# The down product of a mixture-of-experts layer in three fp32r products, with its weights split anew for each tile

## The chip, the cores and the metric

One Trainium2 chip (trn2), one of its cores, one launch. The metric is the device time of that core in microseconds (us), measured over the whole program. All times here are such device times, or spans of one profiled execution of the program.

## The reference

A block of cross-attention followed by a mixture of experts, all in fp32, over 32 sequences of 112 tokens (3584 tokens) of width 256:

```
x = x + attention(layernorm(x), ctx)          # 16 heads of 64, 375 context rows of 192
h = layernorm(x)
p = softmax(h @ gate_w)                       # 8 experts; the best two per token
for each expert e:
    gate, up = split(h @ gate_up_w[e])        # 256 -> 2 x 512
    out_e = (silu(gate) * up) @ down_w[e]     # 512 -> 256
x = x + sum over the two chosen experts of share * out_e
```

The change touches the last product, `@ down_w[e]`, alone.

## The kernel before

The program has two stages. The first walks over the sequences in pairs (`pair`), with attention, the second layernorm, the router, and a scatter of each token's row, twice, into the `bins` of its two experts in memory. The second (`four_tiles`, from about 1158 us on) walks over 63 tiles of 128 rows; all rows of a tile belong to one expert, whose number is read into registers from the table `tile_expert`. `over_tiles` (L187) writes the first twelve tiles out, then loops four tiles at a time, then writes out the last; each engine runs its own copy of `four_tiles`, and semaphores alone order the engines among each other. On each engine the instructions run in the order in which they are written.

The weights of all experts lie in SBUF. Those of gate and up (`Wgu`) are held in two fp32r parts: a high part (the value rounded to fp32r) and a low part (the remainder). A product of two operands so split is made as three matmuls, high by high, high by low and low by high, all into one accumulator (`split_product`, L1314). `Wd`, the down weights, is held whole, in fp32.

For a tile t the engines do this:

- SyncE (SP) reads the tile's first row from the table and loads its 128 rows (`load_rows`, L567), three tiles ahead.
- TensorE (PE) turns the rows into columns (`turn_rows`, L1573, 2 transposes), ScalarE (ACT) rounds them into `hT_h` (`hi_of_rows`, L905), VectorE (DVE) writes the remainder into `hT_l` (`lo_of_rows`, L1245) and keeps the tile's destinations and shares (`keep_dest`, L1251).
- PE makes gate and up (`gate`, L1593, and `hidden`, L1587), 6 matmuls of 512 columns each, with moving operands addressed by the expert's register.
- ACT takes silu of gate out of PSUM (L923); DVE multiplies it with up into `hid` (L1282).
- PE transposes `hid` (L1622, 4 transposes), DVE copies it out of PSUM as `hidT` (L1274), and PE makes the down product in fp32: four matmul instructions, which the profile shows as eight (L1638).
- ACT scales the result by the token's share into `y_out` (L931), and GpSimd (POOL) adds the rows to the output in memory by an indirect DMA (L779). Each of these waits until the one before has landed, since two tiles can hold the same token.

On PE one pass of the loop, for tile t, has this order: transposes of `hid` of t-1; rows of t+1; up of t; down of t-1; gate of t+1. On ACT: silu of t, rounding of the rows of t+1, `y_out` of t-1. On DVE: copy of `hidT` of t-1, remainder of the rows of t+1, `keep_dest`, `hid` of t. `down_ps`, the accumulator of the down product, is one bank; `gate_ps` and `up_ps` are two banks each, `hidT_ps` and the bank of the turned rows are one each.

The first tiles begin before the router is through with the last two sequences. What is left of them, and the rest of the table of tiles (`tiles_left`, `experts_left`, `rows_left`, L1146 to L1176), is written between the tiles, one piece per tile, at given tile numbers.

Of the kernel before, what the change touches and what calls it, by code (L numbers as in the profile page):

```python
# [201 lines left out]
def attention_and_experts(nc, x, ctx_in, Wq, Wkv, Wproj, bproj, gate_w, gate_up_w, down_w, out):  # L202
# [4 lines left out]
    with ExitStack() as stack:  # L207
# [126 lines left out]
        hid = sb("hid", [P, FF], F32)  # L334
        hidT = sb("hidT", [P, FJ, P], F32)
        y_out = sb("y_out", [P, 2, C], F32)
        plan2_at = place["at"]
# [14 lines left out]
        assert place["at"] <= scratch_at + 2 * NJ * C * 4  # L352
# [55 lines left out]
        gate_made, up_made, silu_done, hid_done = sem("gate_made"), sem("up_made"), sem("silu_done"), sem("hid_done")  # L408
        hidT_made, hidT_done, down_made, y_done = sem("hidT_made"), sem("hidT_done"), sem("down_made"), sem("y_done")
# [35 lines left out]
        def _(sp):  # L445
# [153 lines left out]
        def _(pool):  # L599
# [170 lines left out]
            def four_tiles(i):  # L770
                for k in range(4):
# [10 lines left out]
                    if known(t) and t == 3:  # L782
                        scatter(B - 2, 0, None)
                    if known(t) and t == 7:
# [6 lines left out]
        def _(act):  # L791
# [123 lines left out]

            def four_tiles(i):
                for k in range(4):
                    t = 4 * i + k
                    if there(t, NT):
                        act.wait_ge(gate_made, t + 1)  # L920
                        if not known(t) or t >= 1:
                            act.wait_ge(hid_done, t)
                        nc.scalar.activation(silu[:], gate_ps[k % 2][:], ACT.Silu).then_inc(silu_done, 1)  # L923
                    if there(t + 1, NT) and not (known(t) and t == 0):
                        hi_of_rows(t + 1, (k + 1) % 2)
# [7 lines left out]
                    if known(t) and t == 4:  # L933
                        open_gates(B - 1, C_ps)

# [3 lines left out]
        def _(dve):  # L939
# [328 lines left out]

            def four_tiles(i):
                for k in range(4):  # L1270
                    t = 4 * i + k
                    if there(t - 1, NT):
                        dve.wait_ge(hidT_made, t)
                        nc.vector.tensor_copy(hidT[:].rearrange("p j n -> p (j n)"), hidT_ps[:]).then_inc(hidT_done, 1)  # L1274
                    if there(t + 1, NT) and not (known(t) and t == 0):
                        lo_of_rows(t + 1, (k + 1) % 2)

                        keep_dest(t + 1, 2 * i + (k - 3) // 2 + 1, (k + 1) % 4)
                    if there(t, NT):
                        dve.wait_ge(silu_done, t + 1)  # L1280
                        dve.wait_ge(up_made, t + 1)
# [3 lines left out]
                    if known(t) and t == 1:  # L1285
# [4 lines left out]
                    if known(t) and t == 3:  # L1290
                        keep_hnT(B - 1, C_ps)
                    if known(t) and t == 4:
                        least(B - 1, C_ps)
                    if known(t) and t == 5:
# [382 lines left out]
```

## Time and profile before

| | us |
|---|---|
| median of three runs | 1499.28 (1498.85 to 1500.79) |
| the profiled execution | 1500.38 |
| its span | 1498.6 |
| PE busy in the span | 1461.8 (98%) |
| DVE, ACT, POOL busy | 950.6, 732.1, 550.7 |
| granted clock of PE, mean | 0.994 of full speed |

"Busy" of PE is modelled from pipelined matmuls whose times overlap, so what a group of matmuls costs is better read from the distance between starts, or from its piece in the chain of waits. "PEld" is PE's loading of weights, which overlaps its matmuls. A name with a q behind the engine (PEldq, SPq) is the engine's own queue: register, branch and semaphore instructions and DMA issues, which are not counted as busy. "L931" is line 931 of the kernel.

### The profile page before, as it was taken

How to read it: one execution, taken by the hardware profiler on the slowest of the kernel's cores; microseconds unless marked ns; L12 is line 12 of the kernel's file. 1: busy time of each engine (PE TensorE's matmuls, PEld its weight loads, DVE VectorE, ACT ScalarE, POOL GpSimd, SP SyncE). 2: the span in 40 equal slices, each digit the busy share in tenths (PEclk: the TensorE clock that was granted, in tenths of full speed). 3: DMA queues.
4: the chain of work that ended last, by engine and by line, in shares of the span. 5: the costliest groups of instructions: out<-in, count | busy, mean ns of one | idle time of the engine just before them, and what ended most of it. 6: DMA issues, size and time to landing. Idle time of an engine off the chain costs nothing.

```text
span 1498.6 us, 37285 instructions
## 1 busy us (share of the span) xinstructions
PE 1461.8 (98%) x11882; PEld 1289.0 (86%) x11883; DVE 950.6 (63%) x2600; ACT 732.1 (49%) x2032; POOL 550.7 (37%) x641
## 2 busy tenths in 40 slices
PE   6999999999999999999999999999997999999997
PEld 5888889888888988898889888888886888888886
DVE  5667777677767776767777777767668543333332
ACT  4555555555555555555555555555556322222221
POOL 3424334343434343433334343434354332233222
PEclk9999999999999999999999999999998999999999
DMA  9222222222222222222222222213027233333332
GB/s 253 86 66 68 74 73 72 68 73 66 72 72 72 75 92 80 76 72 66 72 73 72 69 72 66 76 40 108 29 80 260 56 59 54 51 49 50 52 53 25
DMA packets 101105, 113.80 MB, mean 76 GB/s; under 512 B 17244, under 2 KB 88140, under 8 KB 101068
## 3 DMA queue, kind: packets, MB, share of 16 engines
q1 hardware_dynamic: 87900, 94.33, 20.6%
q0 software_dynamic: 12144, 15.66, 6.4%
q10 hardware_dynamic: 1024, 3.34, 0.7%
q8 instruction: 21, 0.34, 0.1%
q14 instruction: 16, 0.13, 0.0%
HBM read 61.37 MB, written 51.93 MB: 76 GB/s over the span
## 4 chain that ended last, share of the span: by engine, by line
PE 94%; DVE 3%; DMA 1%; issue 1%; ACT 0%; POOLq 0%; DVEq 0%; SPq 0%
PE bank L1375 25%; PE bank L1318 17%; PE bank L1444 11%; PE bank L1420 10%; PE bank L1410 9%; PE bank L1638 7%; PE bank L1465 6%; PE bank L1382 4%; PE bank L1622 2%; PE bank L1577 1%; DVE probT L1187 1%; DVE Wgu L1056 1%; PE bank L1492 1%; DMA WqL_whole<-in_L_xattn_Wq 1%; PE bank L1482 0%
## 5 line engine op out<-in xcount | busy, mean ns | idle before, releaser
L844 ACT ACTIVATE prob<-bank,neg_max 112x375 f32<-112x375 f32 x512 | 298.7, 588 | 135.7 <-DVE neg_max L1181 135.7
L1181 DVE TENSOR_REDUCE neg_max<-bank 112x1 f32<-112x375 f32 x512 | 243.7, 538 | 16.0 <-PE bank L1410 15.9
L1420 PE MATMUL bank<-ident,prob 112*125 112x112 f32 x1536 | 214.5, 273 | 2.7 <-ACT prob L844 2.4
L1420 PEld LDWEIGHTS bank<-ident,prob 112*125 112x125 f32 x1536 | 195.9, 188 | 13.8 <-ACT prob L844 4.8
L779 POOL DMA_INDIRECT out<-y_out,dest_now x63 | 98.1, 1557 | 221.6 <-ACT y_out L931 196.5
L1444 PE MATMUL bank<-probT,V 125*64 125x112 f32 x3072 | 176.5, 264 | 1.9 <-DVE probT L1187 1.1
L1318 PE MATMUL bank<-Wgu,hT_h 128*128 x504 | 177.1, 433 | 1.0 <-DVE hT_l L1247 1.0
L1444 PEld LDWEIGHTS bank<-probT,V 125*64 125x64 f32 x3072 | 149.0, 137 | 28.4 <-issue 25.1
L969 DVE TENSOR_TENSOR K_l<-bank,K_h 128x376 fp32r<-128x376 f32 x256 | 140.2, 549 | 51.6 <-ACT K_h L804 45.3
L959 DVE COPY V<-bank 125x512 f32<-125x512 f32 x96 | 66.4, 692 | 137.7 <-PE bank L1382 134.7
L802 ACT COPY V<-bank 125x512 f32<-125x512 f32 x96 | 56.3, 587 | 181.3 <-PE bank L1382 178.7
L682 POOL CAST OT_h<-O_now 128x448 fp32r<-128x448 f32 x64 | 37.3, 583 | 287.9 <-DVE O_now L1033 282.0
L1274 DVE COPY hidT<-bank 128x512 f32<-128x512 f32 x63 | 43.5, 691 | 154.4 <-PE bank L1622 154.4
L804 ACT CAST K_h<-bank 128x376 fp32r<-128x376 f32 x256 | 120.9, 473 | 30.6 <-PE bank L1375 29.0
L1187 DVE COPY probT<-bank 125x336 f32<-125x336 f32 x256 | 121.2, 494 | 0.1
L1638 PE MATMUL bank<-Wd,hidT 128*128 x504 | 119.2, 379 | 1.5 <-DVE hidT L1274 1.5
L850 ACT COPY probT<-bank 125x336 f32<-125x336 f32 x256 | 100.3, 443 | 33.5 <-PE bank L1420 33.0
L931 ACT ACTIVATE y_out<-bank,share_now 128x256 f32<-128x256 f32 x63 | 29.8, 473 | 176.9 <-PE bank L1638 176.9
L1375 PE MATMUL bank<-yA_h,WkH 128*128 128x376 f32 x256 | 99.4, 388 | 13.0 <-DVE WkU L987 13.0
L1638 PEld LDWEIGHTS bank<-Wd,hidT 128*128 128x128 f32 x504 | 95.3, 189 | 17.0 <-issue 2.0
L844 ACT ACTIVATION_READ_ACCUMULATOR prob<-bank,neg_max 112x1 f32 x512 | 108.2, 211 | 0.0
L717 POOL TENSOR_SCALAR std<-mv 112x1 f32<-112x1 f32 x32 | 7.7, 240 | 271.8 <-DVE mv L1050 271.8
(196 smaller groups left out, 3587.8 us busy)
## 6 DMA issues: line engine op xcount, KB each, us to landing
bins<-pad_rows SPq DMA_DIRECT2D x29, 1032.0 KB, 5.8
inv_rows<-sums SPq DMA_DIRECT2D x126, 128.0 KB, 2.8
h_in<-bins SPq DMA_DIRECT2D x63, 129.0 KB, 2.1
Wgu<-in_L_ffn_gate_up_w SPq DMA_DIRECT2D x6, 1024.0 KB, 7.8
y_sb<-in_ctx SPq DMA_DIRECT2D x32, 187.5 KB, 2.6
y_sb<-in_ctx SPq DMA_DIRECT2D x62, 93.8 KB, 2.6
x_sb<-in_x SPq DMA_DIRECT2D x16, 224.0 KB, 2.9
x_res<-in_x SPq DMA_DIRECT2D x32, 112.0 KB, 2.4
```

The costliest lines, as they stand in the source:

```text
L804: nc.scalar.copy(K_h[:, arg, :], src[:, 0:LKE]).then_inc(hi_done, 1)
L844: nc.scalar.activation(prob[:, j, :], S_ps[j][0:LQ, 0:LKV], ACT.Exp, bias=neg_max[:, j:j + 1], accum_out=row_sum[:, head // HB, head % HB: ...
L850: nc.scalar.copy(probT[:, j, :], S_ps[j][0:KR, 0:KT * LQ]).then_inc(probT_second, 1)
L969: nc.vector.tensor_tensor(lo, ps, hi.bitcast(F32), ALU.subtract).then_inc(lo_done, 1)
L1181: nc.vector.tensor_reduce(neg_max[:, j:j + 1], S_ps[j][0:LQ, 0:LKV], AX.X, ALU.max, negate=True).then_inc(max_done, 1)
L1187: nc.vector.tensor_copy(probT[:, j, :], S_ps[j][0:KR, 0:KT * LQ]).then_inc(probT_first, 1)
L1318: last = mm(dst, w, m, start=n == 0, stop=n == len(todo) - 1)
L1375: last = mm(out, w, y, start=begins and n == 0, stop=ends and n == "both")
L1410: last = mm(S_ps[2 * k + r][0:LQ, 0:LKE], w[rows, p, q], m[rows, p, :], start=n == 0, stop=n == len(todo) - 1)
L1420: last = nc.tensor.transpose(S_ps[j][0:KR, t * LQ:t * LQ + LQ], prob[:, j, t * KR:t * KR + KR], ident[0:LQ, 0:LQ])
L1444: last = mm(O_ps[r * DK:r * DK + DK, c:c + LQ], V[:, t, (2 * p + r) * DK:(2 * p + r) * DK + DK], probT[:, 2 * k + r, t * LQ:t * LQ + LQ], ...
L1638: last = mm(down_ps[:, 0:C], hidT[:, j, :], Wd[:, experts[k], j, :], start=j == 0, stop=j == FJ - 1)
```

## The change

`hidT` and the down weights are split into fp32r parts, and the down product is made by `split_product` (12 matmuls). ACT writes the high part of `hidT` out of PSUM, DVE the low part. Since there is no room for a second copy of all of `Wd`, the tile's expert is split anew for each tile, high part by ACT, low part by DVE, into one of two buffers, `down_even` and `down_odd`, which lie over memory that attention no longer needs. For this both engines read the experts' numbers into registers, four at a time. `hid` is written in place of silu, so silu of a tile waits for the transposes of the tile before.

The order within a pass changes too. PE: rows of t+1; transposes of `hid` of t-1; up of t; gate of t+1; down of t-1. ACT: rounding of the rows of t+1; high part of `hidT` of t-1; silu of t; high part of the weights of t; `y_out` of t-1. DVE: low part of the rows of t+1; low part of `hidT` of t-1; `keep_dest`; `hid` of t; low part of the weights of t. The pieces of the router and of the plan move one tile later. The plan's temporaries (`plan2_at`) move behind `down_even`.

```diff
@@ -331,10 +331,16 @@
         Wgu = sb("Wgu", [P, E, 2, 2, 2 * FF], F32R)
         scratch_at = place["at"]
         silu = sb("silu", [P, FF], F32)
-        hid = sb("hid", [P, FF], F32)
-        hidT = sb("hidT", [P, FJ, P], F32)
+        hidT_h = sb("hidT_h", [P, FJ, P], F32R)
+        hidT_l = sb("hidT_l", [P, FJ, P], F32R)
         y_out = sb("y_out", [P, 2, C], F32)
-        plan2_at = place["at"]
+        down_parts = [None, nc.alloc_sbuf_tensor_at("down_odd", [P, 2, FJ, C], F32R, offset=place["at"])]
+        assert place["at"] + 2 * FJ * C * 4 <= scratch_at + 2 * NJ * C * 4
+        even_at = plan_at + HALF * P * 4
+        down_parts[0] = nc.alloc_sbuf_tensor_at("down_even", [P, 2, FJ, C], F32R, offset=even_at)
+        plan2_at = even_at + 2 * FJ * C * 4
         h_in = nc.alloc_sbuf_tensor_at("h_in", [P, 4, W], F32, offset=h_in_at)
         place["at"] = wd_at
...
@@ -913,16 +920,38 @@
             hi_of_experts(7, E)
             nc.scalar.activation(table[:], ident[:, 0:1], ACT.Silu)
 
+            def experts_from(i):
+
+                c = 4 * i + 1
+                return nc.values_load_multi_w_load_instructions(
+                    tile_expert[0:1, c:c + 4] if known(i) else tile_expert[0:1, bass.ds(c, 4)],
+                    engines=(mybir.EngineType.Activation,), min_val=0, max_val=E - 1)[1]
+
             def four_tiles(i):
+                if known(i) and i == 0:
+                    act.wait_ge(plan, N_PLAN1)
+                experts = experts_from(i)
                 for k in range(4):
                     t = 4 * i + k
+                    if there(t + 1, NT) and not (known(t) and t == 0):
+                        hi_of_rows(t + 1, (k + 1) % 2)
+                    if there(t - 1, NT):
+                        act.wait_ge(hidT_made, t)
+                        if not known(t) or t >= 2:
+                            act.wait_ge(down_made, t - 1)
+                        nc.scalar.copy(hidT_h[:].rearrange("p j n -> p (j n)"), hidT_ps[:]).then_inc(hidT_hi, 1)
                     if there(t, NT):
                         act.wait_ge(gate_made, t + 1)
                         if not known(t) or t >= 1:
-                            act.wait_ge(hid_done, t)
+                            act.wait_ge(hidT_made, t)
                         nc.scalar.activation(silu[:], gate_ps[k % 2][:], ACT.Silu).then_inc(silu_done, 1)
-                    if there(t + 1, NT) and not (known(t) and t == 0):
-                        hi_of_rows(t + 1, (k + 1) % 2)
+                        if known(t) and t == 0:
+                            act.wait_ge(proj_made, B)
+                            act.wait_ge(wd_early, 16)
+                            act.wait_ge(wd_in, 16)
+                        if not known(t) or t >= 2:
+                            act.wait_ge(down_made, t - 1)
+                        nc.scalar.copy(down_parts[k % 2][:, 0], Wd[:, experts[k]]).then_inc(wd_hi, 1)
                     if there(t - 1, NT):
                         act.wait_ge(down_made, t)
                         if not known(t) or t >= 3:
...
-                    if known(t) and t == 4:
+                    if known(t) and t == 5:
                         open_gates(B - 1, C_ps)
+                    if known(t) and t == 11:
+                        act.wait_ge(plan, N_PLAN)
...
             def four_tiles(i):
+                experts = experts_from(i)
                 for k in range(4):
                     t = 4 * i + k
-                    if there(t - 1, NT):
-                        dve.wait_ge(hidT_made, t)
-                        nc.vector.tensor_copy(hidT[:].rearrange("p j n -> p (j n)"), hidT_ps[:]).then_inc(hidT_done, 1)
                     if there(t + 1, NT) and not (known(t) and t == 0):
                         lo_of_rows(t + 1, (k + 1) % 2)
-
+                    if there(t - 1, NT):
+                        dve.wait_ge(hidT_hi, t)
+                        nc.vector.tensor_tensor(hidT_l[:].rearrange("p j n -> p (j n)"), hidT_ps[:],
+                                                hidT_h[:].rearrange("p j n -> p (j n)").bitcast(F32),
+                                                ALU.subtract).then_inc(hidT_done, 1)
+                    if there(t + 1, NT) and not (known(t) and t == 0):
                         keep_dest(t + 1, 2 * i + (k - 3) // 2 + 1, (k + 1) % 4)
                     if there(t, NT):
                         dve.wait_ge(silu_done, t + 1)
                         dve.wait_ge(up_made, t + 1)
-                        nc.vector.tensor_tensor(hid[:], up_ps[k % 2][:], silu[:], ALU.mult).then_inc(hid_done, 1)
-                    if known(t) and t == 0:
+                        nc.vector.tensor_tensor(silu[:], up_ps[k % 2][:], silu[:], ALU.mult).then_inc(hid_done, 1)
+                        dve.wait_ge(wd_hi, t + 1)
+                        nc.vector.tensor_tensor(down_parts[k % 2][:, 1], Wd[:, experts[k]],
+                                                down_parts[k % 2][:, 0].bitcast(F32), ALU.subtract).then_inc(wd_lo, 1)
+                    if known(t) and t == 1:
                         residual(NP, B - 1, 1, C_ps)
...
+                    if known(t) and t == 8:
                         tiles_left()
-                    if known(t) and t == 8:
+                    if known(t) and t == 9:
                         experts_left()
-                    if known(t) and t == 9:
+                    if known(t) and t == 10:
                         rows_left()
...
                     if known(t) and t == 1:
                         pe.wait_ge(gates_done, B - 1)
                         hidden(up_ps[k % 2][:], experts[k + 1], k % 2, 1).then_inc(up_made, 1)
+                    if there(t + 1, NT) and not (known(t) and t == 0):
+                        turn_rows(i if k < 3 else i + 1, t + 1, (k + 1) % 4)
                     if there(t - 1, NT):
                         pe.wait_ge(hid_done, t)
                         if not known(t) or t >= 2:
                             pe.wait_ge(hidT_done, t - 1)
                         for j in range(FJ):
-                            last = nc.tensor.transpose(hidT_ps[:, j * P:j * P + P], hid[:, j * P:j * P + P], ident[:])
+                            last = nc.tensor.transpose(hidT_ps[:, j * P:j * P + P], silu[:, j * P:j * P + P], ident[:])
                         last.then_inc(hidT_made, 1)
-                    if there(t + 1, NT) and not (known(t) and t == 0):
-                        turn_rows(i if k < 3 else i + 1, t + 1, (k + 1) % 4)
                     if there(t, NT) and not (known(t) and t == 1):
                         if not known(t) or t >= 2:
                             pe.wait_ge(hid_done, t - 1)
                         hidden(up_ps[k % 2][:], experts[k + 1], k % 2, 1).then_inc(up_made, 1)
+                    if there(t + 1, NT):
+                        gate(t + 1, experts[k + 2], (k + 1) % 2)
                     if there(t - 1, NT):
                         pe.wait_ge(hidT_done, t)
-                        if known(t) and t == 1:
-                            pe.wait_ge(wd_early, 16)
-                            pe.wait_ge(wd_in, 16)
+                        pe.wait_ge(wd_lo, t)
                         if not known(t) or t >= 2:
                             pe.wait_ge(y_done, t - 1)
-                        for j in range(FJ):
-                            last = mm(down_ps[:, 0:C], hidT[:, j, :], Wd[:, experts[k], j, :],
-                                      start=j == 0, stop=j == FJ - 1)
-                        last.then_inc(down_made, 1)
-                    if there(t + 1, NT):
-                        gate(t + 1, experts[k + 2], (k + 1) % 2)
-                    if known(t) and t == 2:
+                        parts = down_parts[(k + 1) % 2]
+                        split_product(down_ps[:, 0:C], [(hidT_h[:, j, :], hidT_l[:, j, :], parts[:, 0, j, :], parts[:, 1, j, :])
+                                                        for j in range(FJ)]).then_inc(down_made, 1)
+                    if known(t) and t == 3:
                         count(B - 2)
```

## Rows read from the trace of the kernel before

**Rows 1.** Page of the kernel before: busy time by engine, and the chain's shares.
```profile
PE 1461.8 (98%) x11882; PEld 1289.0 (86%) x11883; DVE 950.6 (63%) x2600; ACT 732.1 (49%) x2032; POOL 550.7 (37%) x641
...
PE 94%; DVE 3%; DMA 1%; issue 1%; ACT 0%; POOLq 0%; DVEq 0%; SPq 0%
```

**Rows 2.** Chain of waits, 1463 to 1499 us: start, duration (us), what.
```profile
1470.54 1.41 PE bank L1318 x6
1471.94 0.44 PE bank L1622 x4
1472.38 0.22 PE bank L1577 x2
1472.60 1.40 PE bank L1318 x6
1474.00 1.73 PE bank L1638 x8
```

**Rows 3.** Page: costliest groups: times | busy us, mean ns | idle before.
```profile
L1638 PE MATMUL bank<-Wd,hidT 128*128 x504 | 119.2, 379 | 1.5 <-DVE hidT L1274 1.5
```

**Rows 4.** Timeline of all engines, 1440 to 1447 us: start, us, engine, line, [idle before].
```profile
1439.61 0.47 ACT L931 ACTIVATE y_out<-bank,share_now 128x256 f32<-128x256 f32 x1 [2.89 <-PE bank L1638]
...
1440.88 0.60 ACT L923 ACTIVATE silu<-bank 128x512 f32<-128x512 f32 x1 [0.79 <-PE bank L1318]
...
1441.32 0.69 DVE L1274 COPY hidT<-bank 128x512 f32<-128x512 f32 x1 [2.81 <-PE bank L1622]
1441.54 0.37 ACT L907 CAST hT_h<-bank 128x256 fp32r<-128x256 f32 x1
...
1441.94 0.42 DVE L1247 TENSOR_TENSOR hT_l<-bank,hT_h 128x256 fp32r<-128x256 f32 x1
```

**Rows 5.** Chain of waits, 608 to 616 us: the output projection.
```profile
611.00 2.85 PE bank L1465 x24
```

**Rows 6.** Instructions of lines 814, 1056 and 684: ns min/median/max, first and last start.
```profile
L814 ACT CAST Wgu<-Wgu x6: 1894/1900/1912, 1128.5 to 1157.2; 128x2048 fp32r<-128x2048 f32 x6
...
L1056 DVE TENSOR_TENSOR Wgu<-Wgu x6: 2281/2292/3037, 1147.0 to 1160.6; 128x2048 fp32r<-128x2048 f32 x6
...
L684 POOL TENSOR_TENSOR OT_l<-O_now,OT_h x64: 1127/1139/3052, 55.5 to 1149.8; 128x448 fp32r<-128x448 f32 x64
```

**Rows 7.** Register loads: PE's queue at line 1583 (1220 to 1222.5 us), SP's at 568.
```profile
L1583 PEldq SEQ_ASSERT  x4: 18/18/18, 1221.2 to 1222.0; - x4
L1583 PEldq TENSOR_LOAD <-tile_expert x1: 338/338/338, 1220.6 to 1220.6; - x1
...
L568 SPq TENSOR_LOAD <-tile_row x2: 265/265/265, 1230.1 to 1235.3; - x2
```

**Rows 8.** Timeline of ACT and DVE, side work in the first tiles.
```profile
1185.47 1.28 ACT L855 ACT_TABLE_LOAD   x1
...
1186.88 0.27 ACT L855 ACTIVATE gates<-bank,neg_top 112x8 f32<-112x8 f32 x1
...
1190.41 0.16 DVE L1073 MAX8 top<-gates 112x8 f32<-112x8 f32 x1
...
1191.69 0.16 DVE L1096 TENSOR_SCALAR dest<-dest 112x2 f32<-112x2 f32 x1
...
1210.33 0.29 DVE L1166 TENSOR_REDUCE prev<-t_tc 128x18 f32<-128x144 f32 x1
...
1212.32 0.18 DVE L1175 SCALAR_TENSOR_TENSOR tile_row<-e_of,within 128x18 int32<-128x18 f32 x1
```

**Rows 9.** Line 779: time from issue to landing; timeline of the last tiles.
```profile
DMA to landing us min/median/max: 3.5/3.8/3.9
...
1487.20 1.56 POOL L779 DMA_INDIRECT out<-y_out,dest_now  x1 [3.42 <-ACT y_out L931]
1489.21 0.47 ACT L931 ACTIVATE y_out<-bank,share_now 128x256 f32<-128x256 f32 x1 [2.82 <-PE bank L1638]
1491.94 1.55 POOL L779 DMA_INDIRECT out<-y_out,dest_now  x1 [3.18 <-issue]
```

More of the change, by code:

```diff
@@ L577, in four_tiles @@
                     t = 4 * i + k
-                    if known(t) and t == 1:
+                    if known(t) and t == 2:
                         sp.wait_ge(x2_done, B)
@@ L781, in four_tiles @@
                             y_out[:, (k + 1) % 2, :], None, compute_op=ALU.add).then_inc(y_store[(k + 1) % 2], 16)
-                    if known(t) and t == 3:
+                    if known(t) and t == 4:
                         scatter(B - 2, 0, None)
-                    if known(t) and t == 7:
+                    if known(t) and t == 8:
                         scatter(B - 1, 1, None)
@@ L1267, in _, with experts_from @@
                 lo_of_expert(e)
+            def experts_from(i):
+                c = 4 * i + 1
+                return nc.values_load_multi_w_load_instructions(
+                    tile_expert[0:1, c:c + 4] if known(i) else tile_expert[0:1, bass.ds(c, 4)],
+                    engines=(mybir.EngineType.DVE,), min_val=0, max_val=E - 1)[1]
             def four_tiles(i):
+                experts = experts_from(i)
                 for k in range(4):
                     t = 4 * i + k
-                    if there(t - 1, NT):
-                        dve.wait_ge(hidT_made, t)
-                        nc.vector.tensor_copy(hidT[:].rearrange("p j n -> p (j n)"), hidT_ps[:]).then_inc(hidT_done, 1)
                     if there(t + 1, NT) and not (known(t) and t == 0):
                         lo_of_rows(t + 1, (k + 1) % 2)
+                    if there(t - 1, NT):
[4 more added lines that the diff above has]
+                    if there(t + 1, NT) and not (known(t) and t == 0):
                         keep_dest(t + 1, 2 * i + (k - 3) // 2 + 1, (k + 1) % 4)
@@ L1281, in four_tiles @@
                         dve.wait_ge(up_made, t + 1)
[L1282 to L1283 removed]
+                        nc.vector.tensor_tensor(silu[:], up_ps[k % 2][:], silu[:], ALU.mult).then_inc(hid_done, 1)
[3 more added lines that the diff above has]
+                    if known(t) and t == 1:
                         residual(NP, B - 1, 1, C_ps)
[L1285 removed]
+                    if known(t) and t == 2:
                         choose(B - 2)
                         mark(B - 2, 0)
[L1288 removed]
+                    if known(t) and t == 3:
                         assign(B - 2, 0)
[L1290 removed]
+                    if known(t) and t == 4:
                         keep_hnT(B - 1, C_ps)
[L1292 removed]
+                    if known(t) and t == 5:
                         least(B - 1, C_ps)
[L1294 removed]
+                    if known(t) and t == 6:
                         choose(B - 1)
                         mark(B - 1, 1)
[L1297 removed]
+                    if known(t) and t == 7:
                         assign(B - 1, 1)
[L1299 removed]
+                    if known(t) and t == 8:
                         tiles_left()
[L1301 removed]
+                    if known(t) and t == 9:
                         experts_left()
[L1303 removed]
+                    if known(t) and t == 10:
                         rows_left()
```

14 lines of the change are left out of this document (6 added, 8 removed).

## The prediction

> **What bounds the kernel now.** I read the page first: TensorE (PE) carries 98% of the span and 94% of the chain [rows 1]. So the question is what PE does per expert tile, and whether anything else ever makes it wait. The chain of waits over the expert stage answers the first half: it never leaves PE, and repeats the five pieces of [rows 2] at each tile. Gate 1.41, transposes of hid 0.44, transposes of the next rows 0.22, up 1.40, down 1.73: 5.20 us (5.18 to 5.19 from start to start). The down product has eight matmuls per tile, 504 in 63 tiles [rows 3]. The timeline of the other engines shows how far they are from PE: VectorE (DVE) idles 2.8 us before it copies hidT, ScalarE (ACT) 2.9 us before y_out [rows 4]. PE is the bound; a cheaper down product comes through in full, as long as the new order leaves PE fed.
>
> **The down product.** Removed: eight fp32 passes, 1.73 us [rows 2]. Added: twelve matmuls of 256 columns on fp32r parts. The output projection is the same form: 24 in 2.85 us, 0.119 each [rows 5], so 1.42 for twelve. Its weights have 112 columns, those here 128; the transposes of hid load 128 columns for each matmul and keep a pace of 0.11 [rows 2], so weight loading does not set the pace. Bounds: 0.11 each (1.32) and 0.216 as now (2.59, if fp32r brought nothing). I take 1.42: 0.31 less per tile. It holds for tiles 0 to 60 (61 times): **-18.9 us**. The new tile is 4.88 us.
>
> **New work on ACT and DVE.** hidT is now rounded by ACT (512 columns, as silu: 0.60) and the remainder taken by DVE (0.69, as the copy it replaces) [rows 4, 6]. The down weights: 1024 columns. Between silu's 0.597 for 512 and the 1.900 for 2048 on ACT a straight line gives 1.03; between DVE's 0.691 and 2.281 it gives 1.22 [rows 4, 6]. ACT then works 0.37+0.60+0.60+1.03+0.47 = 3.07 us of 4.88, DVE 0.42+0.69+0.69+1.22 = 3.02 and two copies of one column. Enough room by sum; what counts is the order.
>
> **One tile, from the end of the down product (time 0).** y_out takes ACT to 0.49. The rows' transposes are out at 0.22, so ACT rounds the rows 0.53 to 0.90, DVE subtracts 0.94 to 1.36 (0.47, 0.37 and 0.42 from [rows 4]). The gate product waits for this. PE arrives there after 0.22+0.44+1.40 = 2.06, its first matmul some 0.15 earlier because matmuls overlap: **0.5 us of slack**. Before, gate stood behind down and had 1.73 more. Then hidT: ACT 0.93 to 1.53, DVE 1.57 to 2.26, needed by down at 3.4; silu to 2.15, rounded weights to 3.2, hid 2.5 to 3.2, weight remainder 3.25 to 4.5, needed in the next tile at 3.4. Slack above 1 us everywhere else. The up product wants hid of the tile before last, long done. PE's new wait for the weight remainder has the whole next tile queued behind it, but the remainder is three us early; ACT's new waits for the down product of the tile before last are met before it comes to them. silu now waits for the transposes of hid (one buffer): out at 0.66, costs nothing.
>
> **Register loads.** Every four tiles ACT and DVE must fetch four expert numbers. PE's own group runs from 1220.6 to 1222.0, 1.4 us; SP's loads have 0.265 instead of 0.338 us for the fetch itself [rows 7]. On DVE it hides behind the weight remainder. On ACT it stands ahead of the rounding of rows, the one chain with little slack. If ACT's queue runs on while y_out computes, rounding starts at some 1.3 to 1.6 instead of 0.53, and PE waits 0.3 to 0.6; if it only starts after y_out, 1.1; if ACT does it for free, 0. I take 0.45, since each of these loads is a queue instruction and y_out's wait is behind the queue by then. There are 15 such starts (t = 4 to 60): **+6.7 us**, bounds 0 and +16.5. The Trainium skill, "DMA: Bandwidth & Descriptors", Latency and other measured facts, gives such a fetch a floor of about 600 ns; by it the wait would be about 0.7, an estimate, and the sum 4 us more. The trace has fetches of 0.265 and 0.338, below that floor, and they decide.
>
> **Side work in the first tiles.** The changes of tile number keep each piece where its input is made. DVE has 1.3 us before the next rows plus the 0.5 of slack, so pieces up to 1.8 us fit. The eight steps for rows_left, 2.17 us [rows 8], do not: 0.3 late. The exponential for the last sequence needs another table: load 1.28 and 0.27 of work between y_out and the rounding of rows [rows 8]: gate waits 1.0. Silu's own load follows, the weight remainder ends 2.5 us later than usual, and choose with mark (1.44 from first to last [rows 8]) stands behind it and ahead of the next rows: 1.3 more. DVE's register loads behind assign, twice: 0.9 together. Sum **+3.5 us**, bounds +1 and +6. Start: gate of tile 2 now covers the splitting of hidT of tile 0, so that the first down loses a wait: -0.3. The wait for Wd moves from PE to ACT, 6 us earlier, its transfer was issued ahead of those of the last experts that ACT had already split; no cost.
>
> **End.** Tile 61's down must wait for the two steps of hidT with only up (1.40) before it: +0.1. The last tile's chain is longer by ACT's 0.6 and shorter by down's 0.3, but the last scatter starts 4.74 us after the one before (1487.20 to 1491.94), while y_out was out at 1489.68 [rows 9]. With POOL's usual 0.8 us after y_out, 1.4 us of cover remain, no cost.
>
> **Sum.** -18.9 + 6.7 + 3.5 - 0.3 + 0.1 = -8.9 us. The profiled execution took 1500.4 (span 1498.6), so it would take 1491.5; the median of the runs is 1499.3, 1.1 lower, hence **1490.4**.
>
> **Rivals.**
> Full gain (25%): ACT's queue loads cost nothing, or slack is larger. For it: queues run ahead on PE without a gap in the chain. Against: ACT's wait for the down product blocks its queue first. -18.9+3.5-0.2 = -15.6: 1483.7; with cheap side work 1481.
> Loads in full (12%): each four-tile start costs 1.1 us: -18.9+16.5+3.5-0.2 = +0.9: 1500.2, no change.
> Scatter as the bound (6%): a scatter cycle (3.5 to 3.9 to landing, then about 0.9 to the next start [rows 9]) is 4.74, against 4.88. It caps any further gain at 0.45 per tile; if it took 4.95, -0.24 x 61 = -14.6 before the other terms: 1494.7.
> Slower, by the weight remainder on DVE (10%): its two SBUF inputs hold up POOL, as the 2048-column subtraction of the expert weights may have done to POOL's OT_l (1.14 usually, 3.05 at most, the last one, which ran beside it) [rows 6]. If 1.22 us of it fell on each scatter's descriptors, the cycle would be 5.96 us, 0.77 over today's tile: +47, 1546. It decides from 0.45 us of overlap on. POOL runs from 1.35 to 2.9 of the tile, the remainder from 3.25 to 4.5: 0.35 us apart, so it needs POOL to slip first. The Trainium skill, "SBUF — State Buffer", Who interferes with whom, has a vector instruction with two SBUF inputs contend only with a GpSimd instruction that reads SBUF, and infers that descriptor writing is spared. By that rule this rival costs nothing; no row of before shows such an instruction beside the scatter.
> A milder slower case (5%): another 0.8 us or more in ACT's chain in every tile (waits, addresses from registers) would eat the slack and the 0.31: 1500 to 1515.
> The change not doing what it says (weights loaded no faster than 0.19 each, twelve of them, 2.27 us) is spoken against by [rows 2, 5]; 1%.
>
> **Numbers.** Forecast's own case 41%: 1486 to 1496. Range 1481 to 1501 leaves out the slower rivals and the far edge of the full gain. Measurement of this kernel can tell 0.2%, 3 us. Faster: own case, full gain, scatter and a part of the loads in full, 0.75; within 3 us 0.10, most of the rest of that case; slower 0.15, from the slower rivals.
>
> **What would show it.** The chain: the down product as x12 at 1.42; tiles of 4.88 with one of about 5.3 in four, its wait on gate behind DVE hT_l behind ACT hT_h, behind register loads on ACT's queue. One wait of 1 us after the second table load. ACT copies of Wd near 1.03, DVE near 1.22. Wrong if all tiles are alike; if down's pace is not 0.119; if the scatter's idle time is released by its own landing in most tiles; if scatter instructions grow beyond 1.55.

## The result and the profile after

The changed kernel takes **1513.36 us** (median; 1512.75 to 1513.77) against 1500.03 for the kernel before on the same chip: a ratio of 1.0084, 95% interval 1.0071 to 1.0097. Forecast was 1490.4, range 1481 to 1501. The change makes the kernel slower by 13 us, and the forecast had the wrong sign.

The page of the changed kernel: PE is busy 13 us less than in [rows 1], in a span that is 13 us longer. The gate's matmuls, which waited 1.0 us in all before (its line stands first below, and is L1318 there), now idle 25.2 us for the low part of the rows.

```profile
L1318 PE MATMUL bank<-Wgu,hT_h 128*128 x504 | 177.1, 433 | 1.0 <-DVE hT_l L1247 1.0
```

After:

```profile
PE 1448.6 (96%) x12134; PEld 1285.2 (85%) x12135; DVE 1027.1 (68%) x2664; ACT 813.4 (54%) x2159; POOL 555.9 (37%) x641
...
L1362 PE MATMUL bank<-Wgu,hT_h 128*128 x504 | 167.9, 415 | 25.2 <-DVE hT_l L1278 25.2
...
L1278 DVE TENSOR_TENSOR hT_l<-bank,hT_h 128x256 fp32r<-128x256 f32 x63 | 26.7, 424 | 111.6 <-ACT hT_h L914 109.4
```

The chain of waits shows both halves of the story. `split_product` makes gate, up and down alike (L1362), so one piece now holds twenty-four matmuls: up 1.40, gate 1.40 and down 1.42, together 4.23 us (in run 3 below up and gate alone take 2.81, which leaves 1.42).

```profile
1259.47 0.22 PE bank L1621 x2
1259.68 0.44 PE bank L1668 x4
1260.12 4.23 PE bank L1362 x24
...
1269.42 0.05 ACT y_out L960
...
1269.84 0.91 ACTq L926
...
1271.85 0.38 ACT hT_h L914
1272.26 0.44 DVE hT_l L1278
...
1272.82 3.08 PE bank L1362 x18
```

A tile is 0.22+0.44+4.23 = 4.89 us, against 5.19 in [rows 2]; forecast was 4.88. The down product does what it should. But once in four tiles the chain leaves PE: y_out, then ScalarE's queue (ACTq) at L926, the register loads, then the rounding and the remainder of the rows, and only then gate. From 1251.48, where one such gate starts, to 1272.82 for the next, four tiles take 21.34 us; at 4.88 they would take 19.52. So each passage through the head of the loop costs 1.8 us. Before, four tiles took 20.74.

Most of it is idle time of TensorE, here in the timeline of the passage at 1312 us:

```profile
1315.49 0.73 PE L1362 MATMUL bank<-Wgu,hT_h 128*128 x2 [1.49 <-DVE hT_l L1278]
```

The other 0.3 us stands at no instruction of its own. Gate and down take 3.08 us in the chain behind this wait and 2.82 otherwise, so I read it as the overlap between matmuls that a wait breaks.

What the loads take is in the view of each line, the number of instructions and their minimum/median/maximum ns. ScalarE's line:

```profile
L926 ACTq FUSED_REGOPS  x64: 147/150/170, 1158.5 to 1484.4; - x64
...
L926 ACTq TENSOR_LOAD <-tile_expert x16: 900/912/1117, 1157.4 to 1482.8; - x16
```

and VectorE's:

```profile
L1303 DVEq TENSOR_LOAD <-tile_expert x16: 967/1268/1377, 1160.7 to 1480.6; - x16
```

A fetch is 0.912 us on ScalarE and 1.268 on VectorE. On SP it is 0.265 [rows 7]. The 0.338 of [rows 7] for PE is only one of its two kinds: in the kernel before, its fetches of four numbers take 0.329 to 0.345 us and most of those of two numbers about 0.54; all together give

```profile
L1583 PEldq TENSOR_LOAD <-tile_expert x33: 329/487/615, 1156.2 to 1474.3; - x33
```

The fetch and the register instructions for its four numbers make a group that ends 1.93 us after it begins. It stands wholly behind the start of y_out, and behind the loop's own register work (L192). In the chain of one pass of the loop:

```profile
1312.19 0.04 ACTq L192
...
1312.41 0.07 ACTq L192
...
1312.51 0.91 ACTq L926
...
1314.44 0.04 ACTq L913
```

The down product ends at 1311.94 there, so the fetch begins 0.57 us behind it, and the rounding of the rows 2.58 us behind it. The last pass is written out, and all but one of the loop's instructions are gone from it. Its down product ends at 1482.46, and the fetch begins 0.32 us behind it:

```profile
1482.71 0.04 ACTq L192
...
1482.78 0.91 ACTq L926
```

That long tile is 1.4 us too long and not 1.8: y_out of tiles 58 and 59 come 6.11 us apart, and 4.74 where run 4 below has no loads.

The first tiles are slow too. Reading y_out in the timeline of each kernel: it comes for tile 0 at 1170.78 (before: 1169.11), for tile 10 at 1226.69 (before: 1221.78). Ten tiles at the new pace should have taken 49 us and took 56.

```profile
1170.43 0.42 DVE L1074 TENSOR_TENSOR x<-bank,x_bias 112x256 f32<-112x256 f32 x1
...
1171.87 0.25 POOL L724 TENSOR_SCALAR std<-mv 112x1 f32<-112x1 f32 x1 [20.28 <-DVE mv L1081]
...
1176.09 1.69 POOL L786 DMA_INDIRECT out<-y_out,dest_now  x1 [0.17 <-issue]
```
```profile
1180.69 1.22 DVE L1325 TENSOR_TENSOR down_odd<-Wd,down_odd 128x1024 fp32r<-128x1024 f32 x1
...
1180.83 2.53 POOL L786 DMA_INDIRECT out<-y_out,dest_now  x1 [3.05 <-DVE share_now L1287]
```

The residual of the last sequence, one tile later than before, holds up GpSimd's (POOL's) normalisation by 6.7 us (std at 1171.87; before 1165.13), and the first scatter with it: 1176.09 against 1170.52. The second scatter begins just behind the weight remainder on VectorE (L1325) and takes 2.53 us instead of 1.55. So do the two after it (2.57 and 2.52).

VectorE's own register loads stand in the chain as well, ahead of the remainder of the rows. They take 1.95 us here (1182.66 to 1184.61), and 1.93 once more from 1206.29 on:

```profile
1182.66 0.84 DVEq L1303
...
1184.66 0.42 DVE hT_l L1278
```

The end gains nothing. Behind tile 60 the last two y_out come 1.2 us sooner than before, but the scatters are behind: the last one starts 4.0 us after the last y_out instead of 2.7, and the chain closes over two landings in a row. From y_out of tile 60 to the end it is 17.9 us, before 17.7.

```profile
1494.92 4.25 DMA out<-y_out,dest_now
...
1500.05 3.77 DMA out<-y_out,dest_now
```

### The profile page after: what moved, and what is told of

Same layout as the page of the kernel before. It is cut to its first block and busy times, and to the rows that moved or that the text cites. A ratio compares the mean times of both kernels' runs of the same rounds, so it can differ in the third digit from the quotient of the medians.

```text
span 1511.5 us, 38193 instructions
## 1 busy us (share of the span) xinstructions
PE 1448.6 (96%) x12134; PEld 1285.2 (85%) x12135; DVE 1027.1 (68%) x2664; ACT 813.4 (54%) x2159; POOL 555.9 (37%) x641
## 5 line engine op out<-in xcount | busy, mean ns | idle before, releaser
L1362 PE MATMUL bank<-Wgu,hT_h 128*128 x504 | 167.9, 415 | 25.2 <-DVE hT_l L1278 25.2
L1362 PEld LDWEIGHTS bank<-Wgu,hT_h 128*128 128x128 f32 x504 | 90.3, 191 | 49.6 <-issue 33.4
L1278 DVE TENSOR_TENSOR hT_l<-bank,hT_h 128x256 fp32r<-128x256 f32 x63 | 26.7, 424 | 111.6 <-ACT hT_h L914 109.4
L1362 PE MATMUL bank<-Wgu,hT_l 128*128 x252 | 100.2, 398 | 0.0
```

Of the source, the lines that this page charges most:

```text
L1362: last = mm(dst, w, m, start=n == 0, stop=n == len(todo) - 1)
```

## The experiments

Each run is compared with the kernel before on the same chip (medians of 1499.0 to 1500.5 in all batches).

**1. ScalarE's loads moved.** Behind the first silu of a pass, ahead of the first weight copy:

```diff
-                experts = experts_from(i)
                 for k in range(4):
...
                         nc.scalar.activation(silu[:], gate_ps[k % 2][:], ACT.Silu).then_inc(silu_done, 1)
+                        if k == 0:
+                            experts = experts_from(i)
```

> The changed kernel with one thing moved: ScalarE reads its four expert numbers after the first silu of a pass of four tiles, in front of the first weight copy, instead of ahead of the rounding of rows. Theory A (the register loads at the head of the pass hold up rows, and so gate): the long tile of each four shrinks from 6.66 to about 4.9 us, four tiles take 19.6 instead of 21.32, the sum of 15 passes gives back 24 to 27 us, 1487 to 1490. Rival B (the branch of the loop and what it costs on each engine, or the scatter, makes the long tile): four tiles stay at 21.3, 1513. Rival C (with the loads out of the way the scatter chain or the weight remainder binds): four tiles stop at 20 to 20.7, 1495 to 1505.

Six executions fell in two groups: 1490.38, 1491.01 and 1491.78, and 1525.56, 1526.67 and 1527.64. The lower ones against before: 0.9939 (0.9920 to 0.9959). They are theory A: 22 us come back from moving one read, a little under the 24 to 27 expected. The upper group is a thing of its own, and the profile fell on it. Waits, then the timeline around one scatter:

```profile
DVE dest_now L1287 <- DMA out<-y_out,dest_now: 116.9, 49, 2.8
```
```profile
1301.27 0.15 DVE L1287 CAST dest_now<-h_in 128x1 int32<-128x1 f32 x1 [2.52 <-DMA out<-y_out,dest_now]
...
1302.00 1.22 DVE L1326 TENSOR_TENSOR down_odd<-Wd,down_odd 128x1024 fp32r<-128x1024 f32 x1
...
1302.05 2.59 POOL L786 DMA_INDIRECT out<-y_out,dest_now  x1 [3.02 <-DVE share_now L1288]
```

`keep_dest` (L1287) waits for a landed scatter, then comes hid, then the weight remainder at 1302.00. POOL starts the next scatter from the same landing (1301.24), 0.05 us behind the remainder, and takes 2.59 us. Its cycle is then 5.6 us, the next landing comes late for both again, and the kernel stays there: y_out of tiles 15 to 61 come 5.59 us apart on average (4.9 to 6.4). I call this the lock (theory E in the later expectations). It is the forecast's slower rival, by the very pair of instructions it named.

Which of the two begins first decides it, by hundredths of a microsecond. In run 4 below a scatter begins 0.03 us ahead of the remainder, and both take their usual time:

```profile
1455.28 1.55 POOL L786 DMA_INDIRECT out<-y_out,dest_now  x1 [4.12 <-DVE share_now L1286]
...
1455.31 1.23 DVE L1324 TENSOR_TENSOR down_even<-Wd,down_even 128x1024 fp32r<-128x1024 f32 x1
```

I counted this in the profiles of the changed kernel and of ten runs (all but 6 and 7, where the remainder is in pieces). In 112 cases a scatter began while such a subtraction was running, and it ended 1.41 to 1.45 us after the subtraction, once 1.55. In 352 cases the subtraction began while the scatter was running, and no scatter took over 1.7 us, no remainder over 1.23.

**2. The residual back at tile 0**, all else as in the changed kernel (one tile number in VectorE's list):

```diff
-                    if known(t) and t == 1:
+                    if known(t) and t == 0:
                         residual(NP, B - 1, 1, C_ps)
```

> The changed kernel with the residual and statistics of the last sequence back at tile 0, where they were before. Theory D (written one tile later, they let GpSimd's normalisation and so the first scatter begin 5.6 us later, 1176.1 instead of 1170.5, after which the chain of scatters leads tiles 3 to 8, with three scatters of 2.5 us): first scatter at about 1171.5, no scatter over 1.7 us in the first tiles, 3 to 5 us less in all, 1508 to 1510. Rival (the first tiles are slow by register loads and the table load, the scatter only looks like the releaser): under 1 us, 1513.

1511.12 us (1.0074, 1.0057 to 1.0090), 2.2 less than the changed kernel's own. The first scatter starts at 1171.70 and the next three take 1.55 to 1.58. The mechanism is as stated, its size just under the 3 to 5 expected: behind tile 3 the chain now goes through VectorE's register loads (1180.96 to 1182.91), which stand behind the assignment of the tokens to their bins, so y_out of tile 4 still comes 6.58 us after that of tile 3 (7.77 in the changed kernel).

**3. The old product in the new order:**

```diff
-                        split_product(down_ps[:, 0:C], [(hidT_h[:, j, :], hidT_l[:, j, :], parts[:, 0, j, :], parts[:, 1, j, :])
-                                                        for j in range(FJ)]).then_inc(down_made, 1)
+                        for j in range(FJ):
+                            last = mm(down_ps[:, 0:C], hidT_h[:, j, :].bitcast(F32), parts[:, 0, j, :].bitcast(F32),
+                                      start=j == 0, stop=j == FJ - 1)
+                        last.then_inc(down_made, 1)
```

> The changed kernel, order and splitting kept, but the down product made in fp32 from the two high parts alone (eight passes in place of twelve fp32r matmuls); it leaves out the low parts in the sum. Tells the worth of the product from the cost of the order. If the cheaper product is worth its 0.31 us in each tile: the short tiles grow from 4.88 to 5.19, four tiles from 21.3 to 22.5, 17 to 19 us more, 1531. If the product's gain was not there or is hidden (scatter as the bound): under 5 us more.

1530.99 us (1.0203, 1.0186 to 1.0220): 17.6 us over the changed kernel, and the product is back at 1.73 in the chain.

```profile
1309.53 2.81 PE bank L1362 x12
1312.34 1.73 PE bank L1683 x8
```

So three fp32r products instead of fp32 are worth 17.6 us here, and the rest of the change costs 31. This kernel leaves out the low parts, so it is a measurement and not a version to use.

**4. No loads on ScalarE at all:** `experts_from` left out there, and the high parts taken from a fixed expert's weights, so that the output isn't the layer's:

```diff
-                        nc.scalar.copy(down_parts[k % 2][:, 0], Wd[:, experts[k]]).then_inc(wd_hi, 1)
+                        nc.scalar.copy(down_parts[k % 2][:, 0], Wd[:, k]).then_inc(wd_hi, 1)
```

> The changed kernel without ScalarE's register loads: its high parts are rounded from a fixed expert's weights, so the high parts are those of another expert. Leaves out: the loads and the addressing by register on ScalarE. If the loads alone make the long tile: four tiles at 19.6, within 2 us of the run that only moves them. If moving them costs ScalarE or VectorE something of its own, this one is faster than that by that amount.

1490.01 and 1491.51 us, the same as the lower group of run 1: four tiles take 19.54 us. The loads alone make the long tile, and at their new place they cost nothing. Without them neither the branch of the loop nor the addressing by register shows; the 0.3 us of L192 count only where the loads follow.

**5. Loads late on both engines, residual at tile 0:** runs 1 and 2 together, and VectorE's loads moved from the head of the pass to

```diff
+                        if k == 0:
+                            experts = experts_from(i)
                         dve.wait_ge(wd_hi, t + 1)
```

> Register loads late on ScalarE and on VectorE (there ahead of the weight remainder of the first tile of a pass), and the residual back at tile 0. Every tile should take 4.88 us. Theory E (in the run that only moved ScalarE's loads, half the executions locked into a state in which each scatter starts just behind VectorE's two-input weight remainder, writes its descriptors in 2.5 instead of 1.55 us and so sets tiles of 5.6 us; a scatter that falls 2 us behind its tile gets there): an earlier first scatter makes it rarer but does not rule it out; executions at 1486 to 1489 and some near 1520. Rival (the lock comes from the late first scatter alone): all at 1486 to 1489.

1488.20 to 1493.78 in four executions, median 1491.07 (0.9941, 0.9922 to 0.9960). None locked; in half the executions of run 1 it had. The time is a miss, since 1486 to 1489 was expected. The first y_out comes at 1173.87: VectorE's loads sit between hid and the weight remainder of tile 0 (2.23 us of idle there).

**6. The weight remainder in four pieces,** on top of run 1:

```diff
-                        nc.vector.tensor_tensor(down_parts[k % 2][:, 1], Wd[:, experts[k]],
-                                                down_parts[k % 2][:, 0].bitcast(F32), ALU.subtract).then_inc(wd_lo, 1)
+                        for j in range(FJ):
+                            last = nc.vector.tensor_tensor(down_parts[k % 2][:, 1, j], Wd[:, experts[k], j],
+                                                           down_parts[k % 2][:, 0, j].bitcast(F32), ALU.subtract)
+                        last.then_inc(wd_lo, 1)
```

> The run that only moved ScalarE's loads, with VectorE's weight remainder cut in four instructions of 256 columns in place of one of 1024. Theory E: GpSimd then waits for one piece of 0.4 us at most, a scatter takes 1.55 to 2.0 us, its cycle stays at 4.7 to 5.1, and no execution comes out near 1526: all at 1489 to 1493. Rival F (GpSimd waits for the whole of VectorE's work, or the lock has nothing to do with the remainder, only with landing times): both states stay, 1491 and 1526.

1492.99 to 1493.37 in four executions (0.9953, 0.9937 to 0.9970). No lock, and the longest scatter of the profile is 1.73 us where run 4's is 2.53 (both have the late residual). It is 2 us slower than run 1's lower group. The remainder takes 1.43 us in four pieces and 1.22 in one; that this makes the difference isn't shown. The scatter's line, of run 6:

```profile
L786 POOL DMA_INDIRECT out<-y_out,dest_now x63: 1540/1547/1725, 1175.8 to 1484.4; - x63
```

and of run 4:

```profile
L786 POOL DMA_INDIRECT out<-y_out,dest_now x63: 1540/1547/2527, 1175.4 to 1482.9; - x63
```

**7. Runs 5 and 6 together.**

> Both edits: loads late on both engines, residual back at tile 0, weight remainder in four pieces. By theory E the best of these: 1484 to 1489 in all executions, faster than the kernel before by 0.8 to 1.0 per cent. By rival F two states.

1489.06 to 1494.00, median 1491.66 (0.9938, 0.9921 to 0.9954). This was expected to be the best, at 1484 to 1489, and is not: it is level with run 5. With the residual in place the pieces gain nothing.

**8. The contention by itself.** The kernel before, with one idle subtraction per tile, into memory that attention no longer needs:

```diff
                         nc.vector.tensor_tensor(hid[:], up_ps[k % 2][:], silu[:], ALU.mult).then_inc(hid_done, 1)
+                        if not known(t) or t >= 12:
+                            dve.wait_ge(y_done, t)
+                            nc.vector.tensor_tensor(extra[:], Wd[:, 0:2], Wd[:, 2:4], ALU.subtract)
```

> The kernel before, with one more instruction on VectorE in each tile from 12 on: when y_out is written, subtract 2048 columns of one SBUF tensor from another, result unused, 2.28 us. It lies over the start of the scatter (0.8 us after y_out). Theory E: GpSimd's scatter instruction waits until VectorE is through, 1.55 grows to about 2.9 to 3.1, its cycle to 6.2, tiles of 6.2 us: 1548 to 1555. If descriptor writing does not mind a two-input instruction: 1.55 stays, tiles 5.2 to 5.8 by VectorE's lateness alone, 1500 to 1530.

1527.24 us, one execution. Most scatters grow from 1.55 to between 2.4 and 2.9:

```profile
1403.06 2.29 DVE L1286 TENSOR_TENSOR extra<-Wd 128x2048 f32<-128x2048 f32 x1 [1.77 <-ACT y_out L932]
...
1404.25 2.53 POOL L780 DMA_INDIRECT out<-y_out,dest_now  x1 [3.18 <-DMA out<-y_out,dest_now]
```

VectorE ends at 1405.35 and the scatter 1.43 us later, at 1406.78; in run 1 VectorE ends at 1303.22 and the scatter 1.42 later, at 1304.64. So a scatter that begins behind a subtraction does nearly all of its work after it. My size was too high, since the scatter slid to the back half of the subtraction, and so was the time (1548 to 1555).

The time doesn't measure the contention. The tiles are 5.56 to 5.71 us, and the chain goes through VectorE, which is late with `hidT` because of the extra work; the scatters aren't in it until the last one:

```profile
1408.27 0.48 ACT y_out L932
...
1408.77 1.24 DVE extra L1286
...
1410.98 0.69 DVE hidT L1275
...
1411.81 2.00 PE bank L1642 x8
```

The time lies where the expectation had put it for VectorE's lateness alone (1500 to 1530). What run 8 shows of the contention is the length of the scatters.

**9. As run 5, VectorE's loads of the first pass at its head again.**

```diff
+                if known(i) and i == 0:
+                    experts = experts_from(i)
...
-                        if k == 0:
+                        if k == 0 and not (known(i) and i == 0):
                             experts = experts_from(i)
```

> As the run with loads late on both engines and the residual at tile 0, but VectorE's loads of the first pass are back at its head, where it is idle; in that run they stood between hid and the weight remainder of tile 0, and y_out of tile 0 came at 1173.9 instead of 1170.3. Theory: 3.5 us less, 1485 to 1490 in its undisturbed executions. By theory E (lock between scatter and weight remainder) an execution near 1520 stays possible; if none of 6 or more shows it, the earlier first scatter has made it rare.

**1487.03 us** (1485.55 to 1489.17 in five executions), ratio 0.9912 (0.9899 to 0.9926): the best version, 13 us faster than the kernel before and 26 than the changed one. The median is 4.0 under run 5, near the 3.5 expected, though the two intervals still touch; that this is all due to tile 0 isn't shown, since in the profiled execution the stage itself began 2 us later (first gate 1159.99, in run 5 1157.89).

```profile
L786 POOL DMA_INDIRECT out<-y_out,dest_now x63: 1540/1547/1687, 1174.2 to 1480.5; - x63
...
  DMA out<-y_out,dest_now: 91.2, 28
```

Even here 28 of the 63 scatters wait for the landing of the one before: the scatter chain is right behind PE. In run 4 it is 44 of them, in the changed kernel with its long tiles 9.

**10. `keep_dest` behind the weight remainder,** on top of run 1 (the two lines that call it moved down).

> The run that only moved ScalarE's loads, with keep_dest (which waits for a landed scatter) behind the weight remainder on VectorE instead of ahead of hid. Theory G (the wait in keep_dest ties the remainder's start to the landing, and the next scatter starts from the same landing, so the two fall together each time): the lock goes, all executions at 1489 to 1492. Rival H (overlap alone is enough, a late scatter meets the remainder wherever it is): both states stay, 1491 and 1515 to 1530.

1487.11 to 1490.81 in four executions, median 1489.24 (0.9924, 0.9909 to 0.9940), no lock. This is for theory G. It is no proof: had the lock kept its one in two, four such executions would come one time in sixteen.

**11. Gate behind the down product again,** the loads where the change has them:

```diff
-                    if there(t + 1, NT):
-                        gate(t + 1, experts[k + 2], (k + 1) % 2)
                     if there(t - 1, NT):
                         pe.wait_ge(hidT_done, t)
...
                                                         for j in range(FJ)]).then_inc(down_made, 1)
+                    if there(t + 1, NT):
+                        gate(t + 1, experts[k + 2], (k + 1) % 2)
```

> The changed kernel with gate behind the down product on TensorE again, as before the change; nothing else. Then gate has 1.4 us more slack, enough for most of the loads on ScalarE, but the two steps of hidT (0.6 and 0.7 us) have only up (1.4) and the rows' transposes ahead of down. Theory A: the long tile shrinks to 5.2 to 5.5 us, the others grow to 4.9 to 5.2; four tiles 20.0 to 21.0, 1495 to 1508, faster than the changed kernel. Rival (loads hold up something other than gate): the long tile stays, 1513 or more.

1513.30 us (1.0083, 1.0068 to 1.0099), the same as the changed kernel, where 1495 to 1508 was expected. The tiles did move the way theory A said, from y_out to y_out 5.13, 5.00, 5.29 and 5.94 us. But the long one was to be 5.2 to 5.5, and the sum, 21.36, is outside the 20 to 21 expected. The loads now hold up hidT in place of gate:

```profile
1314.17 0.92 ACTq L926
...
1316.45 0.60 ACT hidT_h L942
1317.07 0.70 DVE hidT_l L1315
...
1317.82 3.08 PE bank L1362 x18
```

**12. Runs 9 and 10 together.**

> The run with loads late after the first pass and the residual at tile 0, with keep_dest behind the weight remainder as well. If nothing but the last scatters and the first tiles is left over the tile of 4.88 us: the same as without it, 1485 to 1490 in every execution. If keeping the destinations late costs the loads of rows or y_out anything: 1 to 5 us more. An execution near 1520 would speak against theory G.

1487.85 us (1487.27 to 1489.34 in five executions), 0.9928 (0.9915 to 0.9942): the same as run 9 within both intervals, and no lock either.

## Why the prediction was wrong

**The down product: right.** 1.42 us and a tile of 4.88 were forecast; 1.42 (4.23 for all three products) and 4.88 to 4.89 came. Forecast -18.9, measured by run 3: -17.6.

**Splitting on ScalarE and VectorE: right.** The weight copies take 1.05 and 1.23 us (forecast 1.03 and 1.22), and of ordinary tiles the chain leaves PE in none. The slack of 0.5 us ahead of gate held.

**Register loads: the step that failed.** The forecast named the place, the chain and the waiting instruction, and priced it at 0.45 us a pass, +6.7 in all, with an upper bound of 1.1 and +16.5. It came to 1.8, and by run 1 to 22.4 us in all: beyond the bound. (Not all fifteen passages count: without the loads, in run 4, y_out of tile 10 comes at 1227.52, no sooner than the changed kernel's 1226.69. Behind tile 10 there are twelve passages of 1.8 and the last of 1.4, 23 us.)

The forecast let ScalarE's queue run on while y_out computes, and it does. It had the rounding of the rows start 1.3 to 1.6 us after the end of the down product; it starts 2.58 us after it. Three things are in that and in the price. The fetch was taken from PE's and SP's rows (0.338 and 0.265) for two engines that had none, and is 0.91 on ScalarE; the group is 1.93 us where I had 1.1 to 1.4. The loop's own register work ahead of it, 0.3 us, was not counted. Nor were the 0.3 us by which gate and down run longer behind a wait. And the upper bound, with nothing to cover the loads, was made from the same group length, so it was no bound on the one thing that no row showed. The Trainium skill, "DMA: Bandwidth & Descriptors", Latency and other measured facts, gives a floor of about 600 ns; I set it aside, because PE and SP fetch faster than that. The trace still goes below the floor on those two engines (0.33 to 0.54 and 0.265), but for ScalarE (0.912) and VectorE (1.268) the page was nearer than my rows. By its figure the forecast would have been about 4 us higher and still of the wrong sign.

**First tiles: right in kind, too small.** The table load and choose gave 1.2 and 1.0 us (forecast 1.0 and 1.3). What was missed is the first of the moved pieces. The residual is what GpSimd's normalisation waits for, and that stands in POOL's queue ahead of the first scatter. I had counted the residual as work on VectorE alone and did not follow the queue behind it. VectorE's loads were put at 0.9 us for both passages; the group is 1.93 to 1.95 us long and stood in the chain each time. Against an ideal of before less 17.6, run 1's lower group is 8.6 us behind, where 3.3 had been forecast. Moving both, in run 9, brought back 4.0 of it; no run splits the rest.

**The sum.** Loads 15.7 too low, first tiles and end 5.3, product 1.3: 22.3, against the 22.2 between +13.3 and -8.9. It has to close, since the middle term is what the other two leave of run 1; it shows the sizes and proves none.

**The slower rival: real, though not what made this kernel slow.** It was given 10% at +47 us. It needs POOL to slip into the remainder's stretch, which the forecast said. In the changed kernel this happens three times in the first tiles. Later, as I read it, the long tile, once in four, gives the scatters time to catch up: none of the 16 executions with a long tile (the changed kernel, runs 2, 3 and 11) locked. With the long tile gone the lock held half of run 1's executions, at +26 us over the kernel before and not +47. A locked scatter grows by 0.96 to 1.05 us and not by the whole 1.22, and its cycle without the delay can be shorter than 4.74 (4.66 in run 9, from 1475.89 to 1480.55). The Trainium skill, "SBUF — State Buffer", Who interferes with whom, has a two-input vector instruction contend only with GpSimd instructions that read SBUF, and infers that descriptor writing is spared. I had taken the scatter for one that only writes descriptors, by which the rival costs nothing; runs 1 and 8 show that it does wait, 1.55 us becoming 2.5. But it waits only at its start: a subtraction that begins 0.03 us or more into a scatter leaves it at 1.55. The indirect DMA reads its row numbers (`dest_now`) from SBUF, and a wait of that read at its start would fit both the rule and the inference. It was not tried.

**What would have shown it.** The forecast asked for tiles that are not alike and a wait of gate on hT_l on hT_h behind register loads. That is what the chain shows; only its length decided the sign.

**What stays open.** How often the lock comes. It held 3 of 6 executions in run 1 and none of 22 in runs 5, 6, 7, 9 and 12, each of which changes something it needs by theory; nor any of four in run 10, nor of two in run 4. Run 4 has the remainder, `keep_dest` and the residual where run 1 has them, and its profile shows a scatter ahead of the remainder by 0.03 us, so single executions may have missed the lock by luck. Why a fetch into registers is slower on ScalarE and VectorE isn't shown by any run. Their fetches differ from PE's not only in the engine: they begin at entry 4i+1 of the table, PE's four at entry 4i, and on VectorE the median is 0.966 us in runs 1, 9 and 11 against 1.268 in the changed kernel. No run gives two engines the same fetch.

## What to carry to other kernels

Price a register load on each engine by a row of that engine, and of the same fetch. Put it where the engine is ahead of those that wait for it, not at the head of the loop: moving one read was worth 22 us, more than the faster product. When a piece of work is moved, follow every queue that waits for its result, also engines that the piece itself never touches. And a stall may be what keeps a kernel stable: before removing one, look at the chain that runs just behind the bound, here the scatters at 4.74 of 4.88 us.

## What the runs showed of the hardware that I had not expected

- The fetch of four words into registers took 0.91 to 0.92 us on ScalarE and 0.97 to 1.29 on VectorE (medians of the kernels), against 0.329 to 0.345 on TensorE. On TensorE the fetch of two words took longer, about 0.54.
- GpSimd's indirect DMA instruction (1.55 us) ended 1.41 to 1.45 us after the end of a VectorE subtraction of two SBUF tensors that had begun before it, in 111 of 112 cases. Where the scatter had begun first, even by 0.03 us, both took their usual time.
- One kernel on one core had two periods, tiles of 4.88 us and of 5.59 on average. Which one an execution takes is set by the order in which two engines start from the same landing, as I read the trace; no run sets that order by itself.
